# A four-layer graph network: segment mean in three 16-bit parts, gathers of both graph convolutions shared 3 to 5, dst one-hots on ACT

## The reference, cut to what matters

```python
def L0(x, edge_index, edge_attr):                    # the segment mean
    dst = edge_index[1]
    sums = segment_sum(edge_attr, dst, nb_node)      # edge_attr is [100000, 16]
    counts = segment_sum(ones, dst, nb_node)
    return sums / where(counts > 0, counts, 1)[:, None]
# L1: two rounds; a network on 48 edge features makes 16x20 weights for each edge,
#     which are applied to x[dst]; mean over src; batch norm
# L2: a linear edge network applied to x[src]; mean over dst; batch norm
def gcn_conv(h, W, b):                               # L3 calls it twice
    hw = h @ W
    msg = hw[row] * (dinv[row] * dinv[col])[:, None] # row = src, col = dst, with self loops
    return segment_sum(msg, col, N) + b
h = tanh(gcn_conv(x, W1, b1)); h = tanh(gcn_conv(h, W2, b2))
```

## Time and profile before

| | us |
|---|---|
| median of 3 runs | 4364.35 (4363.77 to 4371.9) |
| the profiled execution | 4369.29 |
| its span | 4367.5 |
| PE / DVE / ACT / POOL busy | 3568.2 / 3444.2 / 2056.7 / 2951.8 |
| granted clock of PE, mean | 0.906 |

### The profile page before, as it was taken

One profiled execution on the slowest core, in us unless ns is written; L12 is line 12 of the kernel. 1 busy time (PEld: TensorE's weight loads), 2 busy tenths in 40 slices (PEclk: granted clock), 3 DMA queues, 4 the chain that ended last, 5 costly groups with the idle time before them and its releaser, 6 DMA issues.

```text
span 4367.5 us, 92806 instructions
## 1 busy us (share of the span) xinstructions
PE 3568.2 (82%) x27877; PEld 3016.5 (69%) x27878; DVE 3444.2 (79%) x6087; ACT 2056.7 (47%) x2171; POOL 2951.8 (68%) x2849
## 2 busy tenths in 40 slices
PE   3997999999999699999999957777766666666665
PEld 3995888888888477777777757777755555555554
DVE  7667999999999688888888878888756777566676
ACT  0106999999999599999999900000000000000000
POOL 1325777777777477777777657766437777477776
PEclk9999999999999799999999977777668888688887
DMA  4002111111111321111111111111011111111111
GB/s 51 26 19 24 24 24 24 24 24 24 24 24 23 23 29 31 30 31 30 31 30 31 23 29 30 28 27 25 13 22 34 33 33 33 23 34 33 33 33 24
DMA packets 260307, 121.63 MB, mean 28 GB/s; under 512 B 165614, under 2 KB 222450, under 8 KB 260278
## 3 DMA queue, kind: packets, MB, share of 16 engines
q1 hardware_dynamic: 172470, 90.58, 8.5%
q0 software_dynamic: 87808, 30.68, 7.0%
HBM read 119.25 MB, written 1.78 MB: 28 GB/s over the span
## 4 chain that ended last, share of the span: by engine, by line
PE 31%; POOL 30%; issue 21%; DVE 11%; DVEq 2%; DMA 1%; ACT 1%; SPq 1%; POOLq 0%; ACTq 0%
POOL gb L384 15%; POOL gb L374 15%; PE ps L581 9%; PE ps L597 9%; PE ps L512 7%; PE ps L587 2%; DVE oht L1139 2%; DVE oh L881 1%; ACT v L490 1%; DVE xt L970 1%; PE ps L528 1%; DMA gb<-table,idx 1%; PE ps L703 1%; DVE gb L1174 1%; DVE v L1153 1%
## 5 line engine op out<-in xcount | busy, mean ns | idle before, releaser
L384 POOL DMA_INDIRECT gb<-table,idx x1568 | 1615.6, 1030 | 554.6 <-issue 418.1
L374 POOL DMA_INDIRECT gb<-table,idx x1176 | 1256.4, 1068 | 592.1 <-issue 354.0
L581 PE MATMUL ps<-big,oh 128*128 128x290 f32 (+1 forms) x7840 | 1263.5, 308 | 1.6 <-DVE big L1010 1.6
L581 PEld LDWEIGHTS ps<-big,oh 128*128 128x128 f32 x7840 | 1068.9, 190 | 124.7 <-DVE big L1010 2.2
L597 PE MATMUL ps<-w,ht 128*128 128x320 f32 x3136 | 1008.3, 444 | 95.5 <-DVE xt L970 93.9
L451 ACT ACTIVATE oh<-iota_f,src_n 128x640 fp32r<-128x640 f32 x1372 | 1024.7, 815 | 0.0
L454 ACT ACTIVATE oh<-oh,ones 128x2560 fp32r<-128x2560 f32 (+1 forms) x392 | 849.4, 2167 | 12.7
L597 PEld LDWEIGHTS ps<-w,ht 128*128 128x128 f32 x3136 | 557.3, 191 | 356.7 <-DVE xt L970 165.4
L970 DVE TENSOR_TENSOR xt<-ps,gb 128x640 f32<-128x640 f32 x784 | 642.5, 820 | 90.7 <-PE ps L597 25.6
L703 PE MATMUL ps<-tabb,oht 128*128 128x240 bf16 x3920 | 527.7, 294 | 110.2 <-DVE mk L1209 98.2
L978 DVE TENSOR_REDUCE msg<-xt 128x80 f32<-128x1280 f32 (+1 forms) x392 | 580.4, 1481 | 0.0
(11 more groups left out here) (212 smaller groups left out, 2576.5 us busy)
## 6 DMA issues: line engine op xcount, KB each, us to landing
gb<-table,idx POOLq DMA_INDIRECT x2744, 2.3
eat<-in_eat SPq DMA_DIRECT2D x196, 192.0 KB, 2.4
eat<-vtab SPq DMA_DIRECT2D x147, 256.0 KB
ea<-in_edge_attr SPq DMA_DIRECT2D x98, 64.0 KB, 1.8
idx<-in_dst SPq DMA_DIRECT2D x196, 4.0 KB, 1.5
idx<-in_src SPq DMA_DIRECT2D x147, 4.0 KB, 1.5
ea<-in_edge_attr SPq DMA_DIRECT2D x1, 784.0 KB, 19.4
table<-tabb SPq DMA_DIRECT2D x2, 300.0 KB, 4.4
```

The source lines that it names most:

```text
L374: nc.gpsimd.indirect_dma_start(out=gb[:, b, t, 0:tabw[p]], out_offset=None, in_=tabs[p], in_offset=bass.IndirectOffsetOnAxis(ap=idx[:, b, ...
L384: nc.gpsimd.indirect_dma_start(out=gb[:, b, t, 0:tabw[p]], out_offset=None, in_=tabs[p], in_offset=bass.IndirectOffsetOnAxis(ap=idx[:, b, ...
L581: mm = nc.tensor.matmul(out, oh5[:, b, t, c * P:(c + 1) * P], big[:, b, t, 0:W], start=False, stop=False, skip_group_check=True)
```

## The change

The mean: each value is split into three bf16 parts (high, middle, low) instead of two fp32r parts, so a tile's moving operand is 49 columns in 16 bits. Four pairs (`R`) are in flight. For each pair ACT copies twice and POOL subtracts twice, 256 columns each. DVE makes 16-bit one-hots of a single group and block in one instruction of 128x1024, from node numbers in fp16 (`iota_h`, shifted by `MID`) into a ring of four (`oh_f`). PE's windows are those of single groups (8 matmuls).

The convolutions: every group has 3 tiles (`GP`) gathered by POOL into a ring of four, and 5 (`PT`) by PE. The comparison on DVE is 640 columns wide. The dst one-hots are made on ACT, 8 Abs of 128 columns and one Relu of 1024 in a window, into the ring of four. A window has 3 matmuls of 48 columns and 15 of 80, and PE reads one window entry for a group. SP refills per group.

The pieces below stand on POOL, ACT, PE (`mean_step` to `step(i, r, ahead)`) and DVE, in this order.

`vals`, `ea16`, `iota_h` and the ring lie in memory that the later stages use for other things, so `iota_h` is made again before the convolutions and `dst_f` is shifted there and back.

```diff
-            def split_low(s, b, n):
-                pool.wait_ge(ea_cp, s + 1)
-                nc.gpsimd.tensor_tensor(vals[:, n, :, D + 1:2 * D + 1], ea16[:, b, :, :],
-                                        vals[:, n, :, 0:D].bitcast(F32), ALU.subtract).then_inc(ea_lo, 1)
+            def rest_of(j, r):
+                pool.wait_ge(ea_hi, j + 1)
+                nc.gpsimd.tensor_tensor(ea16[:, r, :, :, :], ea16[:, r, :, :, :], vals[:, r, :, :, 0:D],
+                                        ALU.subtract).then_inc(ea_rest, 1)
+            def low_part(j, r):
+                pool.wait_ge(ea_mid, j + 1)
+                nc.gpsimd.tensor_tensor(vals[:, r, :, :, 2 * D + 1:3 * D + 1], ea16[:, r, :, :, :],
+                                        vals[:, r, :, :, D + 1:2 * D + 1], ALU.subtract).then_inc(ea_lo, 1)
...
+            for p in (3, 4):
                 pool.wait_ge(s_tab, 16 * (p + 1))
...
+                def gather_ring(i, r):
+                    pool.wait_ge(sc_done[p], i * R + r + 1)
+                    gather(p, r, i + 1)
...
+            for p in (3, 4):
+                def window_onehots(i, r):
+                    s = i * R + r
+                    lo, hi, off = load_window(act, s)
+                    with act.Fori(lo, hi) as c:
...
+                        turn = act.snap((off + c) & (R - 1), min_val=0, max_val=R - 1)
+                        act.wait_ge(of_used[p], off + c + 1)
+                        act.sem_inc(s_turn, 1)
+                        for t in range(T):
+                            oh = oh_f[:, bass.ds(turn, 1), t, :].rearrange("p o n -> p (o n)")
+                            nc.scalar.activation(oh, iota_h[:, bass.ds(c * P, P)], ACT.Abs,
+                                                 bias=dst_f[:, bass.ds(s, 1), t], scale=-1.0).then_inc(of_abs[p], 1)
+                        act.wait_ge(of_abs[p], (off + c) * T + T)
+                        act.sem_inc(s_turn, 1)
+                        oh = oh_f[:, bass.ds(turn, 1), :, :].rearrange("p o t n -> p (o t n)")
+                        nc.scalar.activation(oh, oh, ACT.Relu, bias=ones[:, 0:1], scale=-1.0).then_inc(of_ready[p], 1)
...
+            def mean_step(j, r):
+                bounds = [load_window(pe, j * 2 + b) for b in range(2)]
+                pe.wait_ge(ea_lo, j + (R + 1))
+                for b in range(2):
+                    lo, hi, off = bounds[b]
+                    with pe.Fori(lo, hi) as c:
...
+                        turn = pe.snap((off + c) & (R - 1), min_val=0, max_val=R - 1)
+                        pe.wait_ge(om_ready, off + c + 1)
+                        for t in range(T):
+                            mm = nc.tensor.matmul(psf[:, bass.ds(c * 64, 3 * D + 1)],
+                                                  oh_f[:, bass.ds(turn, 1), t, :].rearrange("p o n -> p (o n)"),
+                                                  vals[:, r, b, t, 0:3 * D + 1], start=False, stop=False, skip_group_check=True)
+                        mm.then_inc(om_used, 1)
...
+                def gather_tiles(s, b):
+                    pe.wait_ge(oht_done[p], s * NC + NC)
+                    for g in range(3):
+                        pe.wait_ge(mk_done[p], s * 3 + (g + 1))
+                        for t in range(2 * g, min(2 * g + 2, PT)):
+                            for c in range(NC):
+                                mm = nc.tensor.matmul(ps[:, 5 + g, (t % 2) * GW:(t % 2 + 1) * GW],
+                                                      oht[:, b, c, t * P:(t + 1) * P], tabc[:, c, :, :],
+                                                      start=(c == 0), stop=(c == NC - 1), skip_group_check=True)
+                        mm.then_inc(gm_done[p], 1)
...
+                def scatter_tiles(at, ohs, r):
+                    for t in range(T):
+                        if t < GP:
+                            mm = nc.tensor.matmul(psf[:, bass.ds(at, 3 * D)], ohs(t), gr[:, r, t, 0:3 * D // 2].bitcast(BF16),
+                                                  start=False, stop=False, skip_group_check=True)
+                        else:
+                            for n in range(3):
+                                mm = nc.tensor.matmul(psf[:, bass.ds(at, AW)], ohs(t), mk[:, r % 2, t - GP, n * AW:(n + 1) * AW],
+                                                      start=False, stop=False, skip_group_check=True)
+                    return mm
...
+                def step(i, r, ahead):
+                    s = i * R + r
+                    if ahead:
+                        gather_tiles(s + 1, 1 - r % 2)
+                    lo, hi, off = load_window(pe, s)
+                    pe.wait_ge(g_in[p][r], (i + 1) * 16 * GP)
+                    pe.wait_ge(mk_done[p], s * 3 + 6)
...
+                        pe.wait_ge(of_ready[p], off + c + 1)
+                        scatter_tiles(sums_of(c), lambda t: oh_f[:, bass.ds(turn, 1), t, :].rearrange("p o n -> p (o n)"), r)                            .then_inc(of_used[p], 1)
+                    idle_matmul().then_inc(sc_done[p], 1)
...
+                def step(i, r, more):
+                    s = i * R + r
+                    if more:
+                        tile_onehots(s + 2, r % 2, i * 2 + (r // 2 + 2), False)
+                    if more or r == 0:
+                        select_rows(s + 1, 1 - r % 2)
...
+                    link(V.tensor_scalar(iota_h[:, :], iota_f[:, :], -float(MID), None, ALU.add))
+                    link(V.tensor_scalar(dst_f[:, :, :], dst_f[:, :, :], -float(MID), None, ALU.add))
+                    dve.sem_inc(s_shift, 1)
```

More of the change, by code:

```diff
@@ L38 @@
 EH = 64
+GP = 3
+PT = T - GP
+MID = NP_ // 2
+R = 4
+ROUNDS = NSUP // R
 MP = [2 * (MF + 1), 2 * D]
@@ L46 @@
 BIAS = NB - 1
[L47 removed]
+assert PAIRS % 2 == 1 and NSUP % 2 == 0 and NSUP % R == 2 and EP >= E and NP_ > N
 def repeat(ap, axis, n):
@@ L747, in _ @@
+                    idle_matmul().then_inc(sc_done[p], 1)
+                gather_tiles(0, 0)
+                with pe.Fori(0, ROUNDS) as i:
+                    for r in range(R):
+                        step(i, r, True)
+                for r in range(2):
+                    step(ROUNDS, r, r == 0)
                 idle_matmul().then_inc(s_accd, 1)
@@ L859, in _ @@
             link(V.tensor_tensor(rv, rv, bc(rnf, 3), ALU.mult))
-            def window_onehots(w, s):
-                lo, hi, off = load_window(dve, s)
-                with dve.Fori(lo, hi) as c:
-                    c = nc.s_assert_within(c, 0, NB - 1, skip_runtime_bounds_check_because="a block index out of the window table")
-                    for h in range(2):
-                        dve.wait_ge(oh_used[w][h], off + c + 1)
-                        d = dst_f[:, bass.ds(s, 1), h * 4:h * 4 + 4].rearrange("p o t -> p (o t)")
-                        cols = repeat(iota_f[:, bass.ds(c * P, P)], 1, T // 2)
-                        V.tensor_tensor(oh_b[:, h, :, :], bc(d, P), cols, ALU.is_equal).then_inc(oh_ready[w][h], 1)
             def one_sup(ap3, s):
@@ L882, in pair_onehots @@
                                         ALU.is_equal).then_inc(oh_ready[w][h], 1)
-            with dve.Fori(0, PAIRS) as i:
-                pair_onehots(0, i)
+            with dve.Fori(0, NSUP) as s:
+                lo, hi, off = load_window(dve, s)
+                with dve.Fori(lo, hi) as c:
+                    c = nc.s_assert_within(c, 0, NB - 1, skip_runtime_bounds_check_because="a block index out of the window table")
+                    turn = dve.snap((off + c) & (R - 1), min_val=0, max_val=R - 1)
+                    dve.wait_ge(om_used, off + c + 1)
+                    oh = oh_f[:, bass.ds(turn, 1), :, :].rearrange("p o t n -> p (o t) n")
+                    V.tensor_tensor(oh, bc(one_sup(dst_f, s), P), repeat(iota_h[:, bass.ds(c * P, P)], 1, T),
+                                    ALU.is_equal).then_inc(om_ready, 1)
             def layer_norm(xx):
@@ L952, in _ @@
             dve.sem_inc(s_node, 1)
+            link(V.tensor_scalar(dst_f[:, :, :], dst_f[:, :, :], float(MID), None, ALU.add))
             for l in range(2):
@@ new lines, in step @@
+                def step(i, r, more):
+                    s = i * R + r
+                    if more:
+                        tile_onehots(s + 2, r % 2, i * 2 + (r // 2 + 2), False)
+                    if more or r == 0:
+                        select_rows(s + 1, 1 - r % 2)
+                for b in range(2):
+                    tile_onehots(b, b, 1, True)
+                select_rows(0, 0)
+                with dve.Fori(0, ROUNDS) as i:
+                    for r in range(R):
+                        step(i, r, True)
@@ L1223, in _ @@
+                for r in range(2):
+                    step(ROUNDS, r, False)
             for p in range(2, 5):
```

300 lines of the change are left out of this document (154 added, 146 removed).

## The result

The kernel after took 4341.35 us in the median of 4 runs (4340.7 to 4342.69), the kernel before 4365.78 beside it: ratio 0.9942, 95% interval 0.9925 to 0.9959. It is 24 us faster, not 190, and lies outside the range of 4050 to 4300.

What follows compares the result with a forecast made beforehand. POOL's gathers were taken to bound the convolutions and PE's matmuls the mean. 4369.3 less 49 (mean), 71 and 75 (convolutions), plus 5, gave 4179 us for the profiled execution, 4175 for the median; range 4050 to 4300.

Steps and rivals of the forecast that it cites:

- The bound now: Kernel before: POOL's gathers pace the convolutions (537 of 546 us); PE's matmuls bound the mean (busy 258.8 us).
- The mean: Segment mean: 264 us falls to 215, 49 saved, at 4.4 us a pair.
- 264 (no gain): Segment mean: upper end of its forecast, the stage staying at its old time.
- the 4.4 us between sequencer and port: Segment mean, per pair: taken between PE's sequencer (3.9) and DVE and POOL in turns (4.8), making 215 us.
- The convolutions: Both graph convolutions: ACT ends last at 4.6 us a group, PE next; 475 us each, 71 and 75 saved.
- The 22 us for coupling to PE: Convolutions: added to ACT's 453 us because ACT and PE meet over the ring and windows are uneven.
- The rest: Outside the changed stages: iota_h made twice, dst_f shifted three times, ACT's change of table; 5 us more.
- The signs: Profile after: PE's issue gaps in the mean; in convolutions ACT busy over 90%, gathers under 1.02 us, DVE under 75%.
- C: Rival, convolutions: PE's sequencer or a mixed clock decides, 5.2 us a group, 510 us each; kernel 4245 us; 25%.
- E: Rival, segment mean: gains nothing, since POOL's and DVE's turns take 264 us; kernel 4225 us; 6%.
- D: Rival, convolutions: PE stays at 1.2 GHz, 7.1 us a group, 696 us each; kernel slower at 4615 us; 9%.
- B: Rival: Abs overlap more or POOL's 388 decides; convolutions near 400, mean near 200; kernel 4010 us; 14%.

Runs made afterwards that it cites:

- e2_reads: Kernel after, with PE reading every window list of the segment mean twice (98 more reads): 4404.11 us, ratio 1.008.
- e3_dve: Kernel after, with DVE making the mean's one-hots for 4 of 8 tiles, the others zeroed by one more set-up memset: 4417.2 us, ratio 1.011.
- e1_pairs: Kernel after, with the mean's pair windows, fixed one-hot slots and one list read a pair put back: 4297.87 us, ratio 0.9838.
- c1b_dve2: Kernel after, with DVE making 2 of a window's 8 dst one-hots in the convolutions and ACT 6: 4300.28 us, ratio 0.9839.
- v2b: v1 with DVE making 3 of a window's 8 dst one-hots instead of 2: 4258.31 us.
- c2b_gp2: Kernel after, with a group's gathers in the convolutions shared 2 to POOL and 6 to PE: 4364.09 us, ratio 0.9987.
- v1: Kernel after with the mean of e1_pairs and the convolutions of c1b_dve2: 4248.72 us, ratio 0.9724.
- e4_oldmean: Kernel after with the segment mean of the kernel before, keeping the convolutions of after: 4275.73 us, ratio 0.9786.
- v3b: v1 with one more memset on DVE in the set-up: 4180.66 us, ratio 0.9566.

## Why the prediction was wrong, step by step

**The bound now**: nothing speaks against it. With 98 gathers fewer and L869 off DVE the convolutions got shorter, and a gather took 0.960 us (1.058 before, 0.94 at the low end of the sum). No run moved POOL's gathers alone in the kernel before.

**The mean**: forecast 215, measured 331; this is the step that failed, worth 116 of the 166 us between forecast and result. The mechanism that ends last was named, "What is left on PE is its sequencer", and priced at 191 us; the forecast lay between that and the 235 of the shared port, and the sequencer took more than either. The terms that were mis-sized:
- "eight weight addresses ... at the shortest such step of 0.046 (0.37); eight matmuls at 0.026 (0.21)": the step is 46 ns in its row, but from matmul to matmul it is 0.13 us. The durations of register steps leave out the time to the next step. A window takes 1.99 us instead of 1.07. The earlier trace rows had that distance: 1.32 us of "issue" before the eight matmuls of 48 columns. In the trace of before nine steps lie there, a list read, a turn of the loop and the addresses: 0.95 us long together, they fill 1.45.
- "Two lists ... some 0.5 us each" and the closing matmul: 1.24 in the sum, 2.08 in the timeline, 0.65 of it for a list (e2_reads).
- The upper end, "264 (no gain)", had no row for it. Nothing in the trace excluded a loss, and it should have been open above.

With 1.99 and 2.08, both from one pair of the timeline, the sum would be 49 x (2.49 x 1.99 + 2.08) = 345 us, close to 331.

The rule of the Trainium skill (GPSIMD Engine Reference, "Specifications": the SBUF interface is shared with VectorE) was weighed for the wrong kernel. In after DVE is idle half the time and halving its work changes nothing (e3_dve), so the 4.4 us between sequencer and port stood on a conflict that decided nothing here. The conflict agrees with the rows of e1_pairs, where both run on: one-hots 1.435 us for 1.229, subtractions 1.619 for 1.236.

**The convolutions**: forecast 475, measured 507 and 506. ACT as the last engine, its 3.55 us a window and Abs and Relu at 0.387 and 1.148 us (0.389 and 1.15 forecast) were right: busy 433.6 for 434. Two terms were short:
- "The sequencer ... hides under the Relu but for some 0.2 us of each group": 50 us where this term had 20. The "0.04 for the wait" of each window, 5 us in all, was 14.9. That is 40 us more, and in part the error of the mean again: steps priced by their durations. The cause of the 50 is read from rows, not tested.
- The 22 us for coupling to PE came out at 5.4 of waiting and some 3 at the stage's ends.

PE's 4.2 us a group was short too, and was the price at the full clock. By the prediction's own 4.7 for a sixth of the time at the lower level, which is what the granted 0.92 comes to, PE stood above ACT's 4.6 on paper. With ACT out of the way a group takes 487 / 98 = 4.97 us (c1b_dve2, v2b; clock 0.95), of which 4.37 are matmuls. So an ACT at the forecast 4.6 us would have met a PE at 4.97, and 475 was out of reach.

**DVE and POOL** at 333 and 282 us busy (343 forecast for DVE) are not in the way: DVE took on 38 us more in c1b_dve2 and the stage still fell, POOL shed 85 in c2b_gp2 and nothing was gained. The rule of the Trainium skill that VectorE takes add and relu (ScalarE: Activation LUTs, "Rules for kernel authors") points the way c1b_dve2 went: a quarter of the one-hots on VectorE was worth 20 us a stage, three eighths no more.

**The rest**: +5 forecast, +3.5 seen ahead of the convolutions; the convolutions and the node steps behind them gave back 14 us more than the stretches show, as counted above.

**The signs** that it named nearly all came: gaps named issue, long subtractions, Abs and Relu, PE waiting for ACT, gathers under 1.02 us, DVE at 66% and the clock at 0.92. Only ACT, busy for 86% of its stage, missed its 90. They were signs of the mechanism, and the mechanism can be right with the time 166 us off.

**The rivals**: C was the nearest, in time (4245) and in mechanism, PE's sequencer deciding by its address steps; I placed it in the convolutions, where it is second, and not in the mean, where it decides. E (no gain in the mean, 4225) had the right stage, but gave POOL's and DVE's turns as the reason, and stopped short of a loss. D did not come: 0.92 of the clock was granted where 0.84 had been. B is out.

## What to carry to other kernels

Price a register step by the distance from one instruction to the next in a place of the trace where such a step stands between them, not by its own duration. A slot taken from a register cost PE a step for every matmul, here 0.074 us against 0.05 for the matmul itself; such a ring pays only if PE waits for something else. Do not trust the engine that a wait is put down to before you have seen in the timeline when that engine was done. And price an added step with no upper end at "no gain" unless a row puts it there.

## What the runs showed of the hardware

The first edge-weight stage has two rhythms, 1069 and 1151 us for identical instructions, each holding itself once settled; the runs of a kernel lie at most 13 us apart on these chips, so they share one. The longer one came in e1_pairs, v1 and v2b, which have the mean's pair windows, and in e3_dve, which has after's windows, DVE's halved instructions and one memset more in the set-up. The shorter one came with pair windows too (before, e4_oldmean), and again when v1 got one memset more (v3b). So neither the pair windows nor the memset decides by itself. The first 20 us of the stage are alike in both. Whether a shift of time or the place of the instructions in the stream chooses was not settled. It is worth 2% of this kernel, more than the change was: compare an edit stage by stage before you believe its total.
